# First binary convolution in four 64x64 tiles of TensorE, with halves of images exchanged by DMA

## The chip, the cores and the metric

One core of one Trainium2 chip runs the program. The metric is the time of one execution on the device in microseconds; smaller is better. The engines are TensorE (PE, with its weight loads as PEld), VectorE (DVE), ScalarE (ACT) and GpSimd (POOL); SyncE (SP) issues nearly all DMAs.

## The reference

The input is x, 8 images of 28x28 pixels with 64 channels, in float32. Four blocks follow each other, each as x = x + block(groupnorm(x)), with 32 groups of two channels per image:

```python
x = x + swin_attention(_gn(x))      # shifted 7x7 windows, 8 heads of width 8, relative position bias, mask
# second block, on v = _gn(x) padded by one pixel:
bin_k = where(kernel > 0, 1, -1); alpha = mean(abs(kernel), axis=(0, 1, 2))
bin_x = where(v > 0, 1, -1);      beta = mean(abs(v), axis=channels)
K = sum of beta over 3x3 / 9
x = x + conv3x3(bin_x, bin_k) * (K * alpha) + bias
x = x + conv3x3(_gn(x), sign(kernel2))
x = x + gated_branch(_gn(x))        # 64 -> 2*128 channels, causal conv of 4 taps, silu, gate, 128 -> 64
```

The change touches the second block (a 3x3 convolution of signs, and the scale K * alpha) and the order of some work around it.

## The kernel before

**Layout.** Two images stand on the 128 partitions: channels of the first on 0 to 63, of the second on 64 to 127. The 8 images are four groups g = 0 to 3 of two images. A group has 784 pixels, in two halves i = 0, 1 of 14 rows (392 columns, one PSUM bank in float32).

**Attention** runs over 16 rows of windows R (four per group), each in two parts p; k = 2R + p. Per k: PE multiplies keys and queries (`scores`, L695: four tiles of 32 rows by 49 columns, on row strips 0, 32, 64, 96 and with outputs on partitions 0 or 64 of two banks), DVE takes maximum and difference (`shift`), PE transposes (`turn`), ACT takes exp, PE multiplies with the values (`values`, L726). Then DVE weighs, PE gathers and projects, DVE adds to x (`residual`). POOL masks the keys (`mask_keys`, L207; at the start DVE does one half of the first mask) and ACT seeds the PSUM banks with the position bias. `filler` is a matmul of zeros whose result nobody reads; the numbers of them behind the loads and behind `proj_v(0)` are written in the code (9 and 6).

**First convolution.** `signs(g)` (DVE, L1108) writes +-0.5 into the padded tile sg1. `conv1(g, i)` (PE, L802 to L811) has 9 taps, each one bf16 matmul of 128x128 weights by 392 columns. The weights w1 are block diagonal: a 64x64 block for each of the two images and zeros elsewhere. Output u = 2g + i goes to bank u % 4.

**Channel sums.** ACT writes the absolute normed values (`absolutes`, L500); POOL adds neighbours in the row (`row_sums`, L323 and L325) and in the column (`box_sums`, L330 and L332) into v2. `channel_sums(g, i)` (PE, L859) multiplies v2 with the block diagonal aw (float32, 392 columns; each float32 matmul stands in the trace as two records). ACT copies the result into ka (`evac_ka`, L541).

**finish1(g, i)** (DVE, L1154 and L1156) multiplies the convolution with ka and adds bias and x. It waits for conv_done and ka_ready. When both halves are done, `layer_moments` gives the statistics of the next norm, PE mixes channel pairs (`mix`, L630 and L631), DVE finishes them (`variances`, L996 to L1001) and POOL takes the inverse root (`rsqrt`, L287 and L289).

**Second convolution.** Its input is split in three bf16 parts. ACT makes part one (`split_a`, L550 and L551), DVE the remainder (`remainder`, L1168), ACT part two (`split_b`, L560 and L562), DVE or POOL part three (`third_part`, L220). SP's DMAs place parts in p12 and p33 (L254, L261). PE runs `conv2_stacked` (L823) and `conv2_third` (L837, L842), with 128x64 weights in pairs that write to partitions 0 and 64 of one bank.

**Order.** Each engine runs its list in the order in which it is written; there is no planner. Behind the attention the lists are PE L862 to L898, DVE L1206 to L1255, ACT L590 to L606 and POOL L406 to L418. Waits are on semaphores that count up. SP issues the loads, then the DMAs of the second convolution from the wait for p1_ready on (L244), then the stores.

Of the kernel before, what the change touches and what calls it, by code (L numbers as in the profile page):

```python
# [11 lines left out]
BF16 = mybir.dt.bfloat16  # L12

P = 128
C = 64
HW = 28
TOK = HW * HW
NG = 4
# [10 lines left out]
HALF = TOK // 2  # L29
HR = HW // 2  # L30
# [20 lines left out]
def program(nc, x_in, xw_in, cst_in, wts_in, late_in, ker1_in, ker2_in, rel_in, out):  # L51
    ctx = ExitStack()
    with ctx:
        def sb(name, shape, dt=F32):
            return ctx.enter_context(nc.sbuf_tensor(name, shape, dt))
# [42 lines left out]
        def col(l, g):  # L98
            return l * NG + g
# [24 lines left out]
        v1 = sb("v1", [P, HW, HW])  # L124
        v2 = sb("v2", [P, NG, HW, HW])
        ka = sb("ka", [P, 2, HALF])

        w2 = sb("w2", [P, NTAP, C], BF16)
        parts = sb("parts", [P, 2, 3, PAD, PAD], BF16)
# [21 lines left out]
        def sems(names):  # L151
            return [sem(n) for n in names.split()]
# [27 lines left out]
        sg_ready, ab_ready, h1_done, h_done, v1_done, box_ready = sems(  # L180
            "sg_ready ab_ready h1_done h_done v1_done box_ready")

        conv_done, ka_done, ka_ready, prod_done, x_done = sems("conv_done ka_done ka_ready prod_done x_done")

        p1_ready, rem_ready, p2_ready, p2_placed, p3_ready = sems("p1_ready rem_ready p2_ready p2_placed p3_ready")
# [47 lines left out]
        @block.sync  # L233
        def _(sp):
            sp.dma_start(xwflat[:, 0, :], xw_in[:, 0, :]).then_inc(ld_x0, 16)
            sp.dma_start(wts[:], wts_in).then_inc(ld_w, 16)
            sp.dma_start(rel[:, 0], rel_in).then_inc(ld_rel, 16)
            sp.dma_start(xwflat[:, 1, :], xw_in[:, 1, :]).then_inc(ld_x1, 16)
            sp.dma_start(xwflat[:, 2:NG, :], xw_in[:, 2:NG, :]).then_inc(ld_x2, 16)
            sp.dma_start(xflat, x_in).then_inc(ld_xu, 16)  # L240
            sp.dma_start(ker1[:], ker1_in).then_inc(ld_k1, 16)
            sp.dma_start(ker2[:], ker2_in).then_inc(ld_k2, 16)
            sp.dma_start(late[:], late_in).then_inc(ld_late, 16)
            for g in range(NG):  # L244

                s = g % 2
                if g >= 2:
                    sp.wait_ge(conv_done, 2 * NG + 2 * (g - 1))
                for part, signal in enumerate((p1_ready, p2_ready)):

                    if part == 0 or g > 0:
                        sp.wait_ge(signal, g + 1)
                        for w in range(2):
                            sp.dma_start(p12[64 * part:64 * part + 64, s, w],  # L254
                                         parts[64 * w:64 * w + 64, s, part]).then_inc(stacked[s], 16)
                if g > 0:

                    sp.wait_ge(p3_ready, g + 1)
                    for row in range(2):
                        for w in range(2):  # L260
                            sp.dma_start(p33[64 * row:64 * row + 64, s, w, 0:PAD - row],  # L261
                                         parts[64 * w:64 * w + 64, s, 2, row:PAD]).then_inc(thirds_stacked[s], 16)
            for g in range(NG):
                for i in range(2):

                    sp.wait_ge(res_ready, 2 * g + i + 1)
                    sp.dma_start(out[:, g, i * HALF:(i + 1) * HALF],
                                 res[:, g, i * HALF:(i + 1) * HALF]).then_inc(stored, 16)
            sp.wait_ge(stored, 16 * 2 * NG)
# [151 lines left out]
        def _(act):  # L421
# [114 lines left out]
            def evac_ka(u):  # L536
                i = u % 2
                act.wait_ge(ka_done, u + 1)
                if u >= 2:
                    act.wait_ge(prod_done, u - 1)  # L540
                act.activation(ka[:, i], bk[4 + i][:, 0:HALF], ACT.Identity).then_inc(ka_ready, 1)  # L541
# [46 lines left out]
                act.activation(sz[:, u % 4], zbank(u)[:, 0:HALF], ACT.Silu).then_inc(sz_ready, 1)  # L588

            evac_ka(0)  # L590
            evac_att(NR - 1)
            evac_ka(1)
            evac_ka(2)
            evac_ka(3)
            absolutes(NG - 1)
# [24 lines left out]
        def _(pe):  # L620
# [12 lines left out]
            def filler(ps, n):  # L633

                for _ in range(n):
                    mm = pe.matmul(ps, idle[:, 0:P], idle[:], start=True, stop=True)
                return mm
# [116 lines left out]

            proj_qk(0)
            proj_v(0)
            filler(ps_t[1], 6)
            pe.wait_ge(init_dve, 2)
            scores(0)
            proj_qk(1)  # L760
# [41 lines left out]
            def conv1(g, i):  # L802
# [7 lines left out]
                                   start=(tap == 0), stop=(tap == NTAP - 1))  # L810
                mm.then_inc(conv_done, 1)  # L811

            def conv2_stacked(g, i):

                if i == 0:
                    pe.wait_ge(stacked[g % 2], stacked_by(g))
                    if g == 0:
                        pe.wait_ge(p2_placed, 2)
                ps = conv_bank(2 * NG + 2 * g + i)
                for tap in range(NTAP):  # L820
                    ky, kx = tap // 3, tap % 3
                    for w in range(2):
                        pe.matmul(ps[64 * w:64 * w + 64, 0:HALF], w2[:, tap],  # L823
                                  p12[:, g % 2, w, ky + i * HR:ky + (i + 1) * HR, kx:kx + HW],
                                  start=(tap == 0), stop=False)
# [27 lines left out]
            def channel_sums(g, i):  # L853
                if i == 0:
                    pe.wait_ge(box_ready, g + 1)
                u = 2 * g + i
                if u >= 2:
                    pe.wait_ge(ka_ready, u - 1)
                pe.matmul(bk[4 + i][:, 0:HALF], aw[:], v2[:, g, i * HR:(i + 1) * HR, :],  # L859
                          start=True, stop=True).then_inc(ka_done, 1)  # L860

            pe.wait_ge(w1_ready, 2)  # L862
            conv1(0, 0)
            values(NP - 1)
            project(NR - 2)
            channel_sums(0, 0)
            gather(NR - 1)
            conv1(0, 1)
            project(NR - 1)
            channel_sums(0, 1)  # L870
            conv1(1, 0)
            conv1(1, 1)
            mix(col(1, NG - 1), 1, nth(1, NG - 1), ps_qk)
            channel_sums(1, 0)
            channel_sums(1, 1)
            mix(col(2, 0), 1, nth(2, 0), ps_qk)
            conv1(2, 0)
            conv1(2, 1)
            channel_sums(2, 0)
            channel_sums(2, 1)  # L880
            mix(col(2, 1), 1, nth(2, 1), ps_qk)
            conv1(3, 0)
            conv1(3, 1)
            pe.wait_ge(w2_ready, 7)
            conv2_stacked(0, 0)
            channel_sums(3, 0)
# [82 lines left out]
        def _(dve):  # L969
# [102 lines left out]
            dve.memset(d[:, :, :, WT:64], 0.0).then_inc(init_dve, 1)  # L1072
            dve.wait_ge(pe_bt, 1)
            dve.tensor_tensor(bt[:], ps_o[:, 0:1], ww("bp"), ALU.add).then_inc(bt_ready, 1)
            dve.wait_ge(ld_x1, 16)
            window_moments(1).then_inc(gn_stats, 1)
            dve.wait_ge(ks_ready, 1)
            mask_keys(dve, 0, 0, 2).then_inc(kex_first, 1)
            dve.wait_ge(bt_ready, 1)
            dve.wait_ge(init_dve, 2)  # L1080
            shift(0)
# [126 lines left out]
            residual(NR - 2)  # L1208
            dve.wait_ge(ld_late, 16)
            finish1(0, 0)  # L1210
            residual(NR - 1)
            dve.wait_ge(res_done, NR)
            moments(g, 1).then_inc(gn_stats, 1)
            finish1(0, 1)
            layer_moments(0, 2)
            variances(col(1, g), 1, nth(1, g), ps_qk)
            signs(g)
# [154 lines left out]
```

## Time and profile before

| | |
|---|---|
| median of 3 runs | 218.71 us (217.41 to 220.54) |
| profiled execution, whole time | 217.4 us |
| its span, first to last instruction | 215.5 us |
| PE, DVE, ACT, POOL busy | 203.2, 154.1, 138.9, 94.8 us |
| HBM read, written | 5.03, 1.61 MB |

The span is cut in three here: loads and first norm (to about 13 us), attention (to about 130 us), and the three other blocks. Busy times overlap between engines; a matmul's record runs on while the next one streams, so that the distance between the starts of matmuls, which the chain of waits shows, tells their price, and not the mean length of one.

### The profile page before, as it was taken

What the parts mean: (1) busy time and instruction counts of PE and PEld (TensorE: products, weight loads), DVE (VectorE), ACT (ScalarE), POOL (GpSimd) and SP (SyncE); (2) the same over time, 40 slices, a digit from 0 to 9 for tenths busy, and PEclk for the clock granted to TensorE, in tenths of its full rate; (3) what the DMA queues carried; (4) which work ended last, traced back from release to release, by engine and by line L of the source; (5) the groups of instructions that cost most, each with busy time, mean ns of one, the idle gap of its engine ahead of it and who ended that gap; (6) DMA issues with size and microseconds to landing.
All of it is one profiled execution on the core that took longest, in us unless ns stands there. A gap on an engine that the chain in (4) does not pass through costs nothing.

```text
span 215.5 us, 6793 instructions
## 1 busy us (share of the span) xinstructions
PE 203.2 (94%) x2734; PEld 143.3 (66%) x2735; DVE 154.1 (71%) x316; ACT 138.9 (64%) x294; POOL 94.8 (44%) x108
## 2 busy tenths in 40 slices
PE   7788999999999999999999998997899999899994
PEld 2356888888888878888788865654566665445441
DVE  4665699977886868878769755999796862625543
ACT  2438598779776987788877762278444364876631
POOL 0349999970325199322792019487435200100000
PEclk9999999999999999999999999999999999999999
DMA  6970000000000000000000000001347700002032
GB/s 211 434 292 0 3 3 6 0 3 5 3 3 3 3 2 3 3 3 3 5 0 3 5 3 0 0 22 24 79 94 171 171 2 0 0 3 75 6 111 106
DMA packets 4701, 10.03 MB, mean 47 GB/s; under 512 B 704, under 2 KB 3520, under 8 KB 4544
## 3 DMA queue, kind: packets, MB, share of 16 engines
q1 hardware_dynamic: 4528, 9.27, 13.6%
q8 instruction: 22, 0.36, 0.7%
q10 hardware_dynamic: 144, 0.34, 0.4%
q14 instruction: 7, 0.06, 0.1%
HBM read 5.03 MB, written 1.61 MB: 31 GB/s over the span
## 4 chain that ended last, share of the span: by engine, by line
PE 75%; ACT 7%; DVE 6%; DMA 4%; POOL 3%; issue 3%; SPq 1%; ACTq 0%; POOLq 0%; DVEq 0%
PE turned L706 12%; PE outs L726 11%; PE scores L695 10%; PE scores L914 5%; PE scores L915 4%; PE qkv L666 4%; PE qkv L676 4%; PE scores L808 4%; PE turned L942 3%; PE scores L823 3%; PE outs L748 2%; PE turned L859 2%; DMA xw<-xw_in 2%; DMA p<-parts 2%; PE scores L932 2%
## 5 line engine op out<-in xcount | busy, mean ns | idle before, releaser
L1035 DVE TENSOR_REDUCE mx<-scores 113x16 f32<-113x784 f32 x32 | 30.9, 965 | 9.5 <-PE scores L695 9.3
L706 PE MATMUL turned<-cst,d 113*113 113x113 f32 x256 | 33.3, 273 | 0.9 <-DVE d L1040 0.9
L706 PEld LDWEIGHTS turned<-cst,d 113*113 113x113 f32 x256 | 27.8, 178 | 8.5 <-issue 7.1
L475 ACT ACTIVATE pt<-turned 113x392 f32<-113x392 f32 x64 | 28.4, 495 | 7.1 <-PE turned L706 5.8
L1040 DVE TENSOR_TENSOR d<-scores,mx 113x784 f32<-113x784 f32 x32 | 31.2, 976 | 1.1
L207 POOL TENSOR_TENSOR kex<-ks,cst 128x784 f32<-128x784 f32 (+1 forms) x16 | 23.2, 1452 | 18.6 <-ACT ks L454 18.5
L726 PEld LDWEIGHTS outs<-vsb,pt 113*49 113x49 f32 x1024 | 26.1, 125 | 6.1 <-issue 2.9
L287 POOL TENSOR_TENSOR rstd<-ve,mhalf 128x1 f32<-128x1 f32 (+1 forms) x15 | 8.7, 578 | 47.5 <-DVE ve L1001 47.3
L445 ACT ACTIVATE scores<-rel 113x784 f32<-113x784 f32 x32 | 26.2, 817 | 5.0 <-DMA rel<-rel_in 3.7
L726 PE MATMUL outs<-vsb,pt 113*49 113x18 f32 x1024 | 29.2, 199 | 0.0
L695 PE MATMUL scores<-kex,qs 32*49 32x196 f32 x512 | 28.2, 332 | 0.0
L465 ACT ACTIVATE vsb<-qkv 49x256 f32<-49x256 f32 x32 | 12.8, 399 | 14.4 <-PE qkv L676 14.3
L1185 DVE SCALAR_TENSOR_TENSOR yy<-su,sz 128x392 f32<-128x392 f32 x16 | 8.2, 563 | 18.5 <-PE turned L942 12.5
L581 ACT ACTIVATE su<-scores,late 128x392 f32<-128x392 f32 x16 | 9.3, 587 | 12.8 <-PE scores L915 12.8
L695 PEld LDWEIGHTS scores<-kex,qs 32*49 32x49 f32 x512 | 14.6, 117 | 4.1 <-issue 0.7
L487 ACT ACTIVATE att<-qkv 64x98 f32<-64x98 f32 x64 | 16.2, 253 | 0.6
L914 PE MATMUL scores<-xs,g 128*128 128x392 f32 x32 | 13.7, 510 | 0.6 <-ACT su L581 0.6
L666 PE MATMUL qkv<-xn,wts 128*128 128x196 f32 x64 | 13.6, 336 | 0.0
L823 PE MATMUL scores<-p,w 128*64 128x392 bf16 x144 | 13.2, 334 | 0.1
L915 PE MATMUL scores<-xs,g 128*128 128x392 f32 x32 | 13.1, 491 | 0.0
L808 PE MATMUL scores<-sg,w 128*128 128x392 bf16 x72 | 13.0, 332 | 0.0
L323 POOL TENSOR_TENSOR h<-ab 128x840 f32<-128x840 f32 x4 | 6.3, 1585 | 14.7 <-ACT ab L500 14.6
(121 smaller groups left out, 365.5 us busy)
## 6 DMA issues: line engine op xcount, KB each, us to landing
p<-parts SPq DMA_DIRECT2D x20, 112.5 KB, 2.3
x<-x_in SPq DMA_DIRECT2D x1, 1568.0 KB, 9.8
out<-res SPq DMA_DIRECT2D x8, 196.0 KB, 1.9
xw<-xw_in SPq DMA_DIRECT2D x2, 392.0 KB, 4.7
xw<-xw_in SPq DMA_DIRECT2D x1, 784.0 KB, 6.6
p<-parts SPq DMA_DIRECT2D x6, 108.8 KB, 2.8
ker<-ker_in SPq DMA_DIRECT2D x2, 288.0 KB, 10.1
late<-late_in SPq DMA_DIRECT2D x1, 417.0 KB, 10.7
```

What stands on the lines that cost most here:

```text
L207: return engine.tensor_tensor(kex[:, par, :, a * WT:b * WT], ks[:, a * WT:b * WT].rearrange("p (o t) -> p o t", o=1).broadcast_to([P, 4, n ...
L445: act.activation(o, i, ACT.Identity).then_inc(seeded, 1)
L475: act.activation(pt[0:WK, k % 2, j].rearrange("p n (w t) -> p n w t", w=2), ps_t[j][0:WK, :].rearrange("p (n w t) -> p n w t", n=4, w=2)[: ...
L666: mm = pe.matmul(ps_qk[:, n * RT:(n + 1) * RT], ww(name), rhs, start=True, stop=True)
L695: mm = pe.matmul(ps_s[p][64 * w:64 * w + WT, j, a * 4 * WT:(a + 1) * 4 * WT], qs[q, R % 2, m:m + WT], kex[q, R % 2, :, m:m + WT], start=Fa ...
L706: mm = pe.transpose(ps_t[j][0:WK, n * P:n * P + WK], d[0:WK, k % 2, h:h + 2, :].rearrange("p a b -> p (a b)")[:, 0:WK], ident[0:WK, 0:WK])
L726: mm = pe.matmul(ps_o[64 * w:64 * w + WT, 18 * n:18 * n + 18], pt[0:WK, k % 2, j, 2 * a + hp, WT * w:WT * w + WT], vsb[0:WK, R % 2, 2 * n ...
L808: mm = pe.matmul(ps[:, 0:HALF], w1[:, tap, :], sg1[:, g, ky + i * HR:ky + (i + 1) * HR, kx:kx + HW], start=(tap == 0), stop=(tap == NTAP - 1))
L914: pe.matmul(bk[w][:, 0:HALF], g12[:, w, 0], t[:, SHF + a:SHF + a + HALF], start=True, stop=False)
L915: pe.matmul(bk[w][:, 0:HALF], g12[:, w, 1], t[:, SHF - 2 + a:SHF - 2 + a + HALF], start=False, stop=True).then_inc(u_done, 1)
L1035: dve.tensor_reduce(top, sc, AXX, ALU.max).then_inc(max_done, 1)
L1040: dve.tensor_tensor(d[0:WK, s].rearrange("p (j m) t -> p j m t", j=2)[:, :, :, 0:WT], sc, top.rearrange("p j (m o) -> p j m o", o=1).broad ...
```

## The change

In the first three groups each image has its convolution in two tiles of 64x64: half i = 0 of image w on rows and outputs 64w to 64w + 63, half i = 1 on the other 64 rows. For that its data must lie on the other image's partitions: two DMAs per group copy the lower halves of the signs (sgx) and two those of the box sums (v2x), each crosswise. `conv1_quad(g)` is 36 matmuls in place of 18, `sums_quad(g)` four in place of two. The zero blocks of w1 and aw are not multiplied. Both halves of a group are signalled together. The fourth group stays as it was. PE's list behind the attention is reordered, DVE's and ACT's have one step moved each, and at the start DVE's half of the first mask moves ahead of the statistics of the second group, with 2 fillers in place of 6.

```diff
@@ -124,6 +124,8 @@
         v1 = sb("v1", [P, HW, HW])
         v2 = sb("v2", [P, NG, HW, HW])
         ka = sb("ka", [P, 2, HALF])
+        sgx = sb("sgx", [P, NG - 1, HR + 2, PAD], BF16)
+        v2x = sb("v2x", [P, NG - 1, HR, HW])
 
         w2 = sb("w2", [P, NTAP, C], BF16)
         parts = sb("parts", [P, 2, 3, PAD, PAD], BF16)
@@ -180,6 +182,8 @@
         sg_ready, ab_ready, h1_done, h_done, v1_done, box_ready = sems(
             "sg_ready ab_ready h1_done h_done v1_done box_ready")
 
+        sg_swapped = sems("sg_swapped0 sg_swapped1 sg_swapped2")
+        box_swapped = sems("box_swapped0 box_swapped1 box_swapped2")
         conv_done, ka_done, ka_ready, prod_done, x_done = sems("conv_done ka_done ka_ready prod_done x_done")
 
         p1_ready, rem_ready, p2_ready, p2_placed, p3_ready = sems("p1_ready rem_ready p2_ready p2_placed p3_ready")
@@ -241,6 +245,15 @@
             sp.dma_start(ker1[:], ker1_in).then_inc(ld_k1, 16)
             sp.dma_start(ker2[:], ker2_in).then_inc(ld_k2, 16)
             sp.dma_start(late[:], late_in).then_inc(ld_late, 16)
+            for g in range(NG - 1):
+                sp.wait_ge(sg_ready, g + 1)
+                for w in range(2):
+                    sp.dma_start(sgx[64 * (1 - w):64 * (2 - w), g], sg1[64 * w:64 * w + 64, g, HR:PAD])\
+                      .then_inc(sg_swapped[g], 16)
+                sp.wait_ge(box_ready, g + 1)
+                for w in range(2):
+                    sp.dma_start(v2x[64 * (1 - w):64 * (2 - w), g], v2[64 * w:64 * w + 64, g, HR:HW])\
+                      .then_inc(box_swapped[g], 16)
             for g in range(NG):
 
                 s = g % 2
@@ -588,8 +601,8 @@
                 act.activation(sz[:, u % 4], zbank(u)[:, 0:HALF], ACT.Silu).then_inc(sz_ready, 1)
 
             evac_ka(0)
+            evac_ka(1)
             evac_att(NR - 1)
-            evac_ka(1)
             evac_ka(2)
             evac_ka(3)
             absolutes(NG - 1)
@@ -754,7 +767,7 @@
 
             proj_qk(0)
             proj_v(0)
-            filler(ps_t[1], 6)
+            filler(ps_t[1], 2)
             pe.wait_ge(init_dve, 2)
             scores(0)
             proj_qk(1)
@@ -810,6 +823,20 @@
                                    start=(tap == 0), stop=(tap == NTAP - 1))
                 mm.then_inc(conv_done, 1)
 
+            def conv1_quad(g):
+                pe.wait_ge(sg_swapped[g], 32)
+                ps = [conv_bank(2 * g + i) for i in range(2)]
+                for tap in range(NTAP):
+                    ky, kx = tap // 3, tap % 3
+                    for i in range(2):
+                        for w in range(2):
+                            q = slice(64 * w, 64 * w + 64) if i == 0 else slice(64 * (1 - w), 64 * (2 - w))
+                            rhs = (sg1[q, g, ky:ky + HR, kx:kx + HW] if i == 0 else
+                                   sgx[q, g, ky:ky + HR, kx:kx + HW])
+                            mm = pe.matmul(ps[i][64 * w:64 * w + 64, 0:HALF], w1[q, tap, q], rhs,
+                                           start=(tap == 0), stop=(tap == NTAP - 1))
+                mm.then_inc(conv_done, 2)
+
             def conv2_stacked(g, i):
 
                 if i == 0:
@@ -859,28 +886,33 @@
                 pe.matmul(bk[4 + i][:, 0:HALF], aw[:], v2[:, g, i * HR:(i + 1) * HR, :],
                           start=True, stop=True).then_inc(ka_done, 1)
 
+            def sums_quad(g):
+                pe.wait_ge(box_swapped[g], 32)
+                if g > 0:
+                    pe.wait_ge(ka_ready, 2 * g)
+                for i in range(2):
+                    for w in range(2):
+                        q = slice(64 * w, 64 * w + 64) if i == 0 else slice(64 * (1 - w), 64 * (2 - w))
+                        rhs = v2[q, g, 0:HR] if i == 0 else v2x[q, g]
+                        mm = pe.matmul(bk[4 + i][64 * w:64 * w + 64, 0:HALF], aw[q, q], rhs, start=True, stop=True)
+                mm.then_inc(ka_done, 2)
+
             pe.wait_ge(w1_ready, 2)
-            conv1(0, 0)
+            conv1_quad(0)
             values(NP - 1)
             project(NR - 2)
-            channel_sums(0, 0)
+            sums_quad(0)
             gather(NR - 1)
-            conv1(0, 1)
+            conv1_quad(1)
             project(NR - 1)
-            channel_sums(0, 1)
-            conv1(1, 0)
-            conv1(1, 1)
+            sums_quad(1)
             mix(col(1, NG - 1), 1, nth(1, NG - 1), ps_qk)
-            channel_sums(1, 0)
-            channel_sums(1, 1)
             mix(col(2, 0), 1, nth(2, 0), ps_qk)
-            conv1(2, 0)
-            conv1(2, 1)
-            channel_sums(2, 0)
-            channel_sums(2, 1)
-            mix(col(2, 1), 1, nth(2, 1), ps_qk)
+            conv1_quad(2)
+            sums_quad(2)
             conv1(3, 0)
             conv1(3, 1)
+            mix(col(2, 1), 1, nth(2, 1), ps_qk)
             pe.wait_ge(w2_ready, 7)
             conv2_stacked(0, 0)
             channel_sums(3, 0)
@@ -1072,10 +1104,10 @@
             dve.memset(d[:, :, :, WT:64], 0.0).then_inc(init_dve, 1)
             dve.wait_ge(pe_bt, 1)
             dve.tensor_tensor(bt[:], ps_o[:, 0:1], ww("bp"), ALU.add).then_inc(bt_ready, 1)
+            dve.wait_ge(ks_ready, 1)
+            mask_keys(dve, 0, 0, 2).then_inc(kex_first, 1)
             dve.wait_ge(ld_x1, 16)
             window_moments(1).then_inc(gn_stats, 1)
-            dve.wait_ge(ks_ready, 1)
-            mask_keys(dve, 0, 0, 2).then_inc(kex_first, 1)
             dve.wait_ge(bt_ready, 1)
             dve.wait_ge(init_dve, 2)
             shift(0)
@@ -1208,10 +1240,10 @@
             residual(NR - 2)
             dve.wait_ge(ld_late, 16)
             finish1(0, 0)
+            finish1(0, 1)
             residual(NR - 1)
             dve.wait_ge(res_done, NR)
             moments(g, 1).then_inc(gn_stats, 1)
-            finish1(0, 1)
             layer_moments(0, 2)
             variances(col(1, g), 1, nth(1, g), ps_qk)
             signs(g)
```

## Rows read from the trace of the kernel before

**Rows 1.** The page: busy time by engine, then granted TensorE clock in 40 slices.

```profile
PE 203.2 (94%) x2734; PEld 143.3 (66%) x2735; DVE 154.1 (71%) x316; ACT 138.9 (64%) x294; POOL 94.8 (44%) x108
...
PEclk9999999999999999999999999999999999999999
```

**Rows 2.** Chain of waits behind the attention: start us, length us, engine, line.

```profile
130.03 0.97 issue
...
132.43 1.53 PE scores L808 x9
134.36 0.66 PE turned L859 x2
...
144.29 1.76 DVE rem L1168
146.58 0.56 POOL rstd L287
...
149.40 2.46 POOL v L332
```

**Rows 3.** Chain again, two rates in the attention (x is the count).

```profile
21.85 0.81 PE scores L695 x16
...
24.08 0.68 PE qkv L666 x4
```

**Rows 4.** DVE timeline, 130 to 158: start, length, line, shapes, [idle before].

```profile
132.90 0.57 DVE L1154 TENSOR_TENSOR scores<-scores,ka 128x392 f32<-128x392 f32 x1 [0.74 <-ACT ka L541]
...
134.40 0.80 DVE L1065 SCALAR_TENSOR_TENSOR x<-outs,bt,x 128x100 f32<-128x100 f32 x4 [0.26 <-PE outs L748]
...
140.21 0.16 DVE L996 TENSOR_TENSOR sg<-qkv,epsv 128x3 f32<-128x3 f32 x1 [0.38 <-PE qkv L631]
...
144.20 1.84 DVE L1168 TENSOR_TENSOR rem<-xf,parts 128x784 f32<-128x784 f32 x1
...
157.87 0.92 DVE L1168 TENSOR_TENSOR rem<-xf,parts 128x784 f32<-128x784 f32 x1
```

**Rows 5.** ACT and POOL timelines, 139 to 149, same columns.

```profile
140.54 1.04 ACT L500 ACTIVATE ab<-x,nmr,rstd 128x784 f32<-128x784 f32 x1 [0.17 <-POOL nmr L289]
...
141.72 1.58 POOL L323 TENSOR_TENSOR h<-ab 128x840 f32<-128x840 f32 x1
143.39 1.83 POOL L325 TENSOR_TENSOR h<-h,ab 128x840 f32<-128x840 f32 x1
```

**Rows 6.** PE timeline, 144 to 152, same columns.

```profile
144.81 3.22 PE L808 MATMUL scores<-sg,w 128*128 128x392 bf16 x18
148.08 1.72 PE L823 MATMUL scores<-p,w 128*64 128x392 bf16 x18
151.91 1.58 PE L859 MATMUL turned<-v,aw 128*128 128x392 f32 x4 [2.12 <-POOL v L332]
```

**Rows 7.** Timelines of the head: PE, then DVE, then POOL.

```profile
1.17 4.55 PE L636 MATMUL scores<-idle 128*128 128x512 bf16 x12 [1.17 <-DVE idle L1006]
...
7.13 2.10 PE L636 MATMUL turned<-idle 128*128 128x512 bf16 x9
...
11.48 1.47 PE L636 MATMUL turned<-idle 128*128 128x512 bf16 x5
12.88 0.88 PE L695 MATMUL scores<-kex,qs 32*49 32x196 f32 x16
...
9.67 1.03 DVE L977 BATCH_NORM_STATS2 st<-xw 128x6 f32<-128x392 f32 x2
...
10.87 1.02 DVE L207 TENSOR_TENSOR kex<-ks,cst 128x392 f32<-128x392 f32 x1
...
10.62 0.84 POOL L207 TENSOR_TENSOR kex<-ks,cst 128x392 f32<-128x392 f32 x1 [2.09 <-ACT ks L454]
```

**Rows 8.** DMA issues of the page, then the SP queue's timeline.

```profile
p<-parts SPq DMA_DIRECT2D x20, 112.5 KB, 2.3
...
157.04 2.67 SPq L261 DMA_DIRECT2D p<-parts  x4
```

30

## The prediction

> **What bounds the kernel now.** I read the page first. TensorE is busy 94% of the span, at a granted clock that shows 9 in every slice [rows 1]. That speaks for a TensorE-bound kernel, and for a change that halves TensorE's work. But busy time is no bound, so the second view is the chain of waits behind the attention [rows 2]. There the chain stays on PE from 131 to 141.7 us (the convolutions, at 1.53 us for nine taps, and the channel sums, at 0.66 us for one half), then leaves it: the first remainder on DVE, an inverse root and the box sums of group 3 on POOL, and only with the channel sums of group 3 back to PE, which had idled 2.12 us for them [rows 6]. Third, the timeline of DVE over the same stretch [rows 4]: from 132.90 us to the remainder at 144.20 us it idles twice only, 0.26 us for a projection and 0.38 us for a mix. So PE and DVE run side by side there, both nearly full, and PE's relief is worth what DVE waited for it. Last the head [rows 7]: fillers of TensorE run to 12.88 us, when the first scores start, though DVE's half of the mask was ready at 10.87 + 1.02 = 11.89 us.
>
> **The tiles.** conv1_quad has 36 matmuls of 392 columns. If the four tiles of a tap stream together, a group costs nine steps of 1.53 / 9 = 0.17 us, so 1.53 us where two halves cost 3.06. The trace before has no 64x64 tile. The nearest rows are the scores: four tiles on four row strips, with outputs on two halves of two banks. Their 16 records take 0.81 us, 0.05 us each, where 128x128 matmuls with the same 196 columns take 0.68 / 4 = 0.17 us each [rows 3]: more than three run at once. Pairs that share all rows and differ in the output half also run together: 18 in 1.72 us [rows 6]. The new tiles combine the two. Bounds: 1.53 us a group if loads and streams overlap as there; 36 x 0.05 = 1.82 us if the pace of the scores is a limit per instruction; 3.06 us if only two run at once; 36 x 0.17 = 6.1 us if none do. I take 1.53 plus 0.1 for a change of tile shape (at the scores' start and end about 0.1 us is left over: 0.81 against four streams of 0.17).
>
> The Trainium skill (TensorEngine Tiling (Array Packing), Gotcha 1: PSUM Pressure) says that different row tiles can't access one PSUM bank at the same time. By that the two tiles of a half, which are on different rows and write one bank, would take turns, and a group would cost 3.06 us again. The trace speaks against it: the scores' tiles of row strips 0 and 32 write two halves of one bank and keep the pace above. It stays as a rival below.
>
> sums_quad has four float32 matmuls; four together cost 0.66 us in place of 1.31 (twice the 0.66 of one half [rows 2]); one after the other they would cost 2.6 us. PE saves 3 x (1.53 + 0.66) = 6.6 us in all, if the tiles work.
>
> **What that moves, on the path.** The first quad stands ahead of values(31), where conv1(0, 0) stood, with the same 1.53 us: no gain, and 0.1 us lost to the change of shape, since the chain goes on to weigh(15) (the 0.97 us of issue at 130.03 us [rows 2] is PE waiting for it). sums_quad(0) ends as channel_sums(0, 0) did, again with 0.1 us of shape change, shared with the first one in my sum since DVE's finish1(0, 0) waits for ka (0.74 us idle [rows 4]): together -0.1 us, at worst -0.4 us at the scores' pace. ACT now copies ka twice before evac_att(15), so project(15) comes some 0.4 us later. DVE needs it only behind finish1(0, 1), 0.57 + 0.63 us later than before, so its wait of 0.26 us goes: +0.26 us. If PE were 0.8 us later still, it would come back. Then the moments of group 3 and of group 0, as before. PE has by then done conv1_quad(1) and sums_quad(1) and idles, so both mixes run as soon as their moments stand, and the 0.38 us wait [rows 4] goes too.
>
> What is late next: POOL. Its row sums for group 3 wait for ACT's absolutes at 140.54 us, which wait for the root of variances(1, 3), ahead of the second wait [rows 5]. They gain the 0.26 us and a little, not the 0.64. DVE's remainder(0) took 1.84 us where an undisturbed one takes 0.92 [rows 4]; it ended at 146.04 us, which is 0.82 us after POOL's second row sum (143.39 + 1.83 = 145.22 us [rows 5]). So it stood still until POOL was done, as two engines that lock each other out would, and an earlier start of it buys nothing: it ends when POOL's sum ends, plus 0.82. Behind it come variances(2, 1), the root, the box sums and the channel sums of group 3 [rows 2], from which on the order is unchanged and PE nearly full. The tail therefore gains what the row sums gain: 0.3 us to 0.4 us, less the 0.1 above. I take 0.3, with bounds -0.1 (shape changes at their upper end, gain of 0.26) and 0.7 (both waits, none lost).
>
> mix(2, 1) moves behind conv1(3). PE: quad(2) from about 139.0, sums to 141.2, conv1(3) to 144.2 with 3.06 us; the mix ends before 145.6, when remainder(0) does. It costs nothing; without that cover it would cost up to 1.4 us less whatever PE is early.
>
> **The DMAs.** Twelve more, in SP's list ahead of the wait for p1_ready. An issue takes 2.67 / 4 = 0.67 us of the queue, a landing 2.3 us [rows 8]. Groups 0 and 1 exchange in the middle of the attention, long before use. The signs of group 2 are ready at 127 us and are used at 139. Its box sums end at 136.5 us: two issues, 1.3 us, and 2.3 us to land make 140.1, and sums_quad(2) is due at about 140.5. SP is then free at 137.9 us, before p1_ready at 143 us, so nothing behind is held. If the landing takes 1 us more, PE's slack before the mix covers it; beyond that, it counts in full. Price zero.
>
> **The head.** Four fillers fewer: 4 x 2.10 / 9 = 0.93 us [rows 7]. The mask: DVE and POOL start their halves together; DVE's took 1.02 us for half the elements of a 0.92 us operation, and ended 0.44 us after POOL's (11.46 us), so here too one waited for the other. Moved ahead, it ends at 11.0 us if DVE comes first, at 11.9 us if POOL does; the two remaining fillers end at 11.95 us. Scores start then, 0.93 us earlier. DVE's statistics of group 1 (1.03 us and 0.2 for merging [rows 7]) now stand between: in the worse case they end at 13.1 us, and shift(0), which began at 13.92, starts at 13.15. So 0.8 us, bounds 0.75 and 0.93. Everything in the attention hangs on that first difference, so it moves along; the loads are long in. Sum: 0.8 + 0.3 = 1.1 us less. Against the profiled execution, 217.4 - 1.1 = 216.3 us. That one equals the fastest of the runs shown; their median is 1.3 us higher, so for the median 218.7 - 1.1 = 217.6 us.
>
> **The rivals.**
> *PE was the bound.* For it: 94% busy [rows 1], and the chain of waits on PE until 141.7 us. Then all 6.6 us and the 0.8 come out: 211.3 us. Against it: DVE's two idles sum to 0.64 us there, and PE already idled 2.12 us for POOL. 5%.
>
> *The tiles take turns* (slower side). Place: conv1_quad(0), ahead of values(31), then sums_quad(0). In two turns: 1.53 us more in front of weigh(15), 0.66 us more in front of finish1(0, 0); 1.53 us more before project(15), of which about 0.8 is covered by DVE. It comes to 1.5 + 0.7 + 0.7 less the 1.1: about 219.5 to 220.5 us. It decides once a quad takes over some 2.3 us, where the gain of the head is used up. None at once: 4.6 + 2.0 + 3.5 - 1.1 = 9 us more, 227.7 us. For it: no row shows the four tiles of this shape. 7% and 3%.
>
> *TensorE's clock falls.* PE's work between 135 and 151 us shrinks to islands: idle from about 135.2 to 137.3, and from mix(2, 1) at 144.6 until p12 is placed, about 147.7 us (conv2_stacked started at 148.08 [rows 6]). That is 3.1 us, beyond the longest idle that rows show at full clock, 2.12 us [rows 6]. At the lower clock, as in the first burst, 12 fillers took 4.55 us where nine later took 2.10 [rows 7]: PE lost 4.55 - 12 x 0.233 = 1.75 us until it rose. conv2_stacked(0, 0) would hide a part. Cost 0.5 to 1.8 us: 218.1 to 219.4 us, and in two gaps up to 222. 9%.
>
> *Head gains nothing*, because some load or POOL's list sets the first rows of the attention: 218.4 us. 6%. The forecast itself has 66%; 4% is for what I don't see.
>
> **Numbers.** Predicted 217.6 us. The runs shown spread over 3 us without any change, so the range takes 2.4 us below (runs like the fastest, and 0.7 for the tail) and 2.2 above (the tiles in two turns, or the clock): 215.2 to 219.8. About 2% (4.4 us) is what a measurement of this kernel can tell from no change. Faster by over 2% is the PE-bound rival and a little: 6%. Slower by over 2% needs the serial tiles, or two falls of the clock: 7%. Within: 87%.
>
> **What would show it.** In the trace after: conv1_quad 36 records in about 1.6 us (3.1: turns); scores(0) at about 11.95 us and DVE's first maximum at 13.0 to 13.2; no idle of DVE for PE between 134 and 144 (shifted by 0.8); row sums of group 3 about 1.1 us earlier than 141.72, remainder(0) again ending 0.8 us behind the second; PE idle of 2 us and more in the islands, at clock 1.00; channel sums of group 3 at about 150.8 us. I would be wrong if POOL and DVE take their lock in another order there (each such swap moves 1 to 2 us either way), or if the swap of group 2 lands after 141 us.

## The result: 0.6% slower, and TensorE's clock fell twice

The kernel after takes 219.4 us, median of 12 runs (218.43 to 220.48), against 218.7 us of before beside it. The ratio is 1.0062, 95% interval 1.0037 to 1.0086: slower, by less than 2%, where 217.6 us and a ratio of 0.995 were forecast. The time lies inside the range of 215.2 to 219.8 us, but it moved the other way than forecast. Medians here count every run; ratios leave out runs over 1.5% above the fastest of their kernel. Its profiled execution took 219.4 us at a span of 217.4 us, 1.9 us more than before's.

The page of the kernel after, its busy row and the granted clock in 40 slices:

```profile
span 217.4 us, 6930 instructions
...
PE 201.3 (93%) x2797; PEld 141.4 (65%) x2797; DVE 153.0 (70%) x316; ACT 138.5 (64%) x294; POOL 94.9 (44%) x108
...
PEclk9999999999999999999999999796699999999999
```

TensorE is busy 1.9 us less [rows 1], and the clock row dips to 7 and then to 6 where before's stays at 9. All 12 runs have a granted clock below 1.00 (0.975 to 0.992). The same stretch of the profiled one read by windows (start and end, length, PE busy and its records, granted clock, share of DMA, GB/s), cut where the clock changes:

```profile
core 0: us, PE busy (x), PEclk, DMA share, GB/s
134.80:138.50 3.70, 1.26 (x16) 1.00 0.25 54
138.50:141.90 3.40, 3.40 (x43) 0.50 0.00 0
141.90:148.70 6.80, 5.00 (x42) 1.00 0.16 34
148.70:155.50 6.80, 4.84 (x20) 0.51 0.17 36
155.50:160.00 4.50, 4.50 (x55) 0.99 0.26 57
```

The clock stands at its lower level (1.2 GHz in place of 2.4) from 138.5 to 141.9 us and from 148.7 to 155.5 us. Ahead of the first fall TensorE did little: 1.26 us of records in 3.7 us, and behind the second conv1_quad's sums those are mixes, whose matmuls have one or two columns. Ahead of the second it waited 1.80 us for x, with a mix before that wait. The timeline of PE shows the islands (behind each row the idle time before it, and who ended it):

```profile
136.63 0.38 PE L643 MATMUL qkv<-mv,cst 128*128 128x2 f32 x2 [1.79 <-DVE mv L1016]
...
137.88 0.35 PE L643 MATMUL qkv<-mv,cst 128*128 128x2 f32 x2 [0.65 <-DVE sg L1028]
...
147.72 2.22 PE L850 MATMUL scores<-p,w 128*64 128x392 bf16 x18 [1.80 <-DVE x L1188]
151.91 2.98 PE L886 MATMUL turned<-v,aw 128*128 128x392 f32 x4 [1.96 <-POOL v L345]
```

No idle is longer than 1.96 us, and that one comes behind the second fall; ahead of the falls stand 1.79 and 1.80 us. Before had 2.12 us [rows 6], which went by at full clock in its profiled execution. The chain of waits behind the attention shows what the low clock did:

```profile
126.63 1.65 PE scores L836 x36
...
138.46 3.00 PE scores L836 x36
141.46 0.96 PE turned L897 x8
...
146.58 0.56 POOL rstd L300
...
151.91 2.98 PE turned L886 x4
```

The first quad (126.63) takes 1.65 us for its 36 matmuls, the third (138.46) 3.00 us for the same. The channel sums follow late, then conv1 of group 3 at full clock. The second fall meets the channel sums of group 3: 2.98 us at 151.91, where before's took 1.58 at the same instant [rows 6]. So everything that the head and the order had gained was gone by 146.58 us, where POOL's root starts at the very time of before's [rows 2], and 1.4 us more went in the channel sums. The rest, to 1.9 us, came with the next matmuls.

The head did what the sum said. First scores, DVE's half of the mask, DVE's first maximum:

```profile
11.95 0.88 PE L708 MATMUL scores<-kex,qs 32*49 32x196 f32 x16
...
10.45 0.57 DVE L211 TENSOR_TENSOR kex<-ks,cst 128x392 f32<-128x392 f32 x1 [0.75 <-ACT ks L467]
...
13.00 0.97 DVE L1067 TENSOR_REDUCE mx<-scores 113x16 f32<-113x784 f32 x1 [0.79 <-PE scores L708]
```

12.88 us became 11.95 [rows 7]. DVE got its mask in first and took 0.57 us in place of 1.02.

### The profile page after: what moved, and what is told of

Read it like the earlier page. It is cut to its first block, busy times and chain, and to the rows that moved or that the text cites. A ratio compares the mean times of both kernels' runs of the same rounds, so it can differ in the third digit from the quotient of the medians.

```text
span 217.4 us, 6930 instructions
## 1 busy us (share of the span) xinstructions
PE 201.3 (93%) x2797; PEld 141.4 (65%) x2797; DVE 153.0 (70%) x316; ACT 138.5 (64%) x294; POOL 94.9 (44%) x108
## 4 chain that ended last, share of the span: by engine, by line
PE 72%; DVE 8%; ACT 7%; issue 4%; POOL 3%; DMA 3%; SPq 1%; DVEq 0%; ACTq 0%; POOLq 0%
PE turned L719 12%; PE outs L739 11%; PE scores L708 10%; PE scores L946 5%; PE scores L947 4%; PE qkv L679 4%; PE qkv L689 4%; PE turned L974 3%; PE scores L836 2%; DMA xw<-xw_in 2%; PE outs L761 2%; PE scores L964 2%; ACT pt L488 2%; PE scores L850 1%; PE scores L821 1%
## 5 line engine op out<-in xcount | busy, mean ns | idle before, releaser
L850 PE MATMUL scores<-p,w 128*64 128x392 bf16 x144 | 13.7, 342 | 1.8 <-DVE x L1188 1.8
L689 PE MATMUL qkv<-wts,xn 128*49 128x64 f32 x256 | 10.3, 222 | 2.6 <-ACT qs L468 2.6
```

The source lines that it names most:

```text
L689: mm = pe.matmul(ps_qk[64 * e:64 * e + WT, a * C:(a + 1) * C], xn[:, R % 3, a], ww("wv")[:, e * C:(e + 1) * C], start=True, stop=True)
```

## The experiments

Each kernel ran in up to five rounds beside the kernel before on the same chip; ratios are to that. "Hold" is this function, which reads zeros and writes a bank nobody reads at that time:

```python
def hold(n):
    pe.wait_ge(res_done, NR)
    for _ in range(n):
        pe.matmul(ps_o[:, 0:384], idle[:, 0:P], idle[:, 0:384], start=True, stop=True)
```

### The clock held, and only that

```diff
             sums_quad(1)
+            hold(7)
             mix(col(1, NG - 1), 1, nth(1, NG - 1), ps_qk)
+            hold(3)
             mix(col(2, 0), 1, nth(2, 0), ps_qk)
...
             mix(col(2, 1), 1, nth(2, 1), ps_qk)
+            hold(12)
             pe.wait_ge(w2_ready, 7)
             conv2_stacked(0, 0)
+            hold(10)
```

> The kernel after, with 32 matmuls of zeros (384 columns, bf16, into a bank nobody reads) put on TensorE where it idles: 7 ahead of the mix of group 3's first-block moments, 3 behind it, 12 ahead of the first conv2_stacked and 10 behind it. Nothing else differs. Theory 1, the clock: the granted clock stays 1.00 from 130 to 160 us, the third conv1_quad takes 1.6 us in place of 2.9, channel sums of group 3 start at about 150.6 us, and the time is about 1.2 us below before (ratio 0.993 to 0.996). Theory 2, the order on DVE and POOL or the 12 DMAs took the time and the clock only came along: the time stays at that of the kernel after (ratio about 1.006), or rises by what the added matmuls delay.

Measured: 215.95 us (215.76 to 216.58), ratio 0.9892 (0.9861 to 0.9924), clock 1.00. The same windows (columns as above):

```profile
134.80:138.50 3.70, 3.09 (x26) 1.00 0.25 54
138.50:141.90 3.40, 3.40 (x51) 1.00 0.00 0
141.90:148.70 6.80, 6.19 (x48) 1.00 0.16 36
148.70:155.50 6.80, 6.41 (x54) 1.00 0.31 68
```

And of its chain of waits the root, the channel sums of group 3, and a later DMA:

```profile
145.38 0.56 POOL rstd L300
...
150.72 1.58 PE turned L886 x4
...
157.64 3.88 DMA p<-parts
```

TensorE does 32 useless matmuls more, and the kernel gets 3.4 us faster than without them (219.4 against 215.95, in two sessions, each with before beside it: 1.0062 against 0.9892). So the falls of the clock are what costs, and theory 2, that the order or the DMAs took the time by themselves, is out. (That the order sets how much a fall costs is shown further down.) The channel sums start at 150.72 us; the prediction's signs had 150.8. The ratio is lower than theory 1 said, 0.993 to 0.996, for a reason that the runs of before give, below: they have falls of their own.

### One stretch at a time

The same kernel with the first two holds alone, and with the last two alone.

> The kernel after with the added matmuls of zeros only in the first stretch (7 ahead of the mix of group 3's first-block moments, 3 behind it). The clock theory: the first fall (138.5 us) goes, the second (148.8 us) stays, clock about 0.984 to 0.992 over the span. If the falls cost about the same, about 216.9 us; if the second is the one that counts, since the channel sums of group 3 and what follows run in it, 217.3 us or more (216.0 with both held, 219.4 with none).

Measured: 217.44 us (215.84 to 218.06), ratio 0.9947 (0.9919 to 0.9974), clock 0.992 in the profiled execution.

> The same with the added matmuls only in the second stretch (12 ahead of the first conv2_stacked, 10 behind it). The first fall stays: third conv1_quad 2.9 us, mix of group 1 behind conv1 of group 3 at 145.4 us, box sums at 147.5 as in the kernel after. The 12 matmuls may then stand in the way, since the stretch begins 1.7 us later. About 217.2 to 217.9 us, clock 0.984.

Measured: 217.56 us (216.52 to 219.03), ratio 0.9954 (0.9927 to 0.9981). Its profiled execution, 218.52 us at a clock of 0.983, was one of the longer ones; nine of the 12 have 0.990 to 0.992. With one fall left, either one, the kernel stands 1.5 us (second left) or 1.6 us (first left) above 215.95; with both, 3.4. So by the medians the falls cost about the same, and they add up. The 216.9 us expected for that case were added wrongly: half of 3.4 us on top of 216.0 makes 217.7. The other case, that the second fall is the one that counts, fits the 217.44 us but not the 217.56.

### As many instructions, no work

```diff
-        pe.matmul(ps_o[:, 0:384], idle[:, 0:P], idle[:, 0:384], start=True, stop=True)
+        pe.matmul(ps_o[:, 0:1], idle[:, 0:P], idle[:, 0:1], start=True, stop=True)
```

> The kernel after with the same 32 added matmuls of zeros in the same places, but one column each in place of 384: as many instructions, almost no streaming. The clock theory: the clock falls twice again, time as the kernel after (ratio 1.004 to 1.008). Rival, the added instructions help by their waits or their places in the list and not by TensorE's work: ratio 0.989 again.

Measured: 218.99 us, ratio 1.001 (0.997 to 1.005). The interval excludes the rival's 0.989 and reaches only the lower end of the clock theory's 1.004 to 1.008. The single times say why: 10 of 12 lie between 218.65 and 220.07 us at a clock of 0.976 to 0.984, as the kernel after, and two at 217.18 and 215.96 us with 0.991 and 0.992, near the held ones. In the profile:

```profile
134.80:138.50 3.70, 1.66 (x21) 0.82 0.25 54
138.50:141.90 3.40, 3.40 (x42) 0.50 0.00 0
...
155.50:160.00 4.50, 4.50 (x42) 0.76 0.24 51
```

The clock is down in the first stretch again, here from 137.2 to 144.0 us, and once more behind 154 us. With one column per matmul the falls stayed, with 384 they went. That rules out the holds' places in the list and their waits as the cause of the gain.

### The head alone

```diff
-            filler(ps_t[1], 6)
+            filler(ps_t[1], 2)
...
-            dve.wait_ge(ld_x1, 16)
-            window_moments(1).then_inc(gn_stats, 1)
             dve.wait_ge(ks_ready, 1)
             mask_keys(dve, 0, 0, 2).then_inc(kex_first, 1)
+            dve.wait_ge(ld_x1, 16)
+            window_moments(1).then_inc(gn_stats, 1)
```

> The kernel before with the head of the change alone: DVE's half of the first mask ahead of the statistics of group 1, and 2 fillers in place of 6. Theory 1: the gain of the head, 0.93 us in the trace of the kernel after, reaches the end when the clock stays up: ratio 0.995 to 0.997, clock 1.00 throughout. Theory 2, something later (POOL's list, a load, the box sums) takes it back: ratio 0.999 to 1.001.

Measured: 216.77 us (216.06 to 218.06), ratio 0.9947 (0.9916 to 0.9978): seven of its 11 runs have a clock of 0.999 or 1.00 and a median of 216.45 us, four have 0.992 and 217.64 to 218.06. Before's runs at full clock beside it have a median of 217.21 us, so the head is worth 0.76 us, of 0.8 forecast. Its profiled execution, at a span of 215.8 us, was one of the four, and slower than before's. Windows, and two rows of PE's timeline:

```profile
145.00:148.70 3.70, 3.65 (x31) 1.00 0.04 9
148.70:152.10 3.40, 1.28 (x7) 0.98 0.29 68
152.10:156.00 3.90, 3.90 (x24) 0.58 0.26 59
```

```profile
151.04 2.14 PE L859 MATMUL turned<-v,aw 128*128 128x392 f32 x4 [2.12 <-POOL v L332]
...
153.75 2.46 PE L842 MATMUL scores<-parts,w2z 128*64 128x392 bf16 x18
```

The idle ahead of the channel sums is 2.12 us, to the hundredth that of before [rows 6], where the clock stayed up; here it fell about 1 us after the idle had ended. So one and the same idle can go either way. The clock didn't stay up throughout, as theory 1 had it, and yet the gain came through.

> The kernel after with the head undone (statistics first, 6 fillers). Theory 1: the clock falls behind the attention as in the kernel after, and the time is 0.9 us above it: ratio to before 1.010. Theory 2, the head's fewer fillers bring the fall of the clock: the clock stays 1.00 and the ratio is 0.998 to 1.000.

This is the kernel after with the head as before. Measured: 220.56 us (219.6 to 222.89), ratio 1.0108 (1.0062 to 1.0154), clock 0.976. Taking the head out costs another 1 us and leaves the falls: the missing fillers are not their cause.

### The two heaps of before

The 12 runs of before beside the kernel after are 217.17 to 217.59 us five times and 218.71 us and more seven times, with nothing between. If the upper heap is one fall of the clock in that idle of 2.12 us, matmuls of zeros there take it away:

```diff
             conv2_stacked(0, 0)
+            hold(10)
             channel_sums(3, 0)
```

> The kernel before with 10 matmuls of zeros (384 columns) behind its first conv2_stacked, where TensorE idles 2.1 us ahead of the channel sums of group 3. The times of before fall in two heaps, near 217.3 and near 218.7 us. Theory: the upper heap is one fall of the clock in that idle; then the held kernel has one heap near 217.3 us and a ratio of about 0.997. Rival: the heaps have another cause; then they stay, ratio 1.000.

Measured: 217.62 us, 12 runs from 217.17 to 218.01, ratio 0.9972 (0.9952 to 0.9993), clock 1.00. Of the 29 runs of before beside it, 14 lie at 217.18 to 217.92 and 15 at 218.66 to 220.47. The upper heap is gone. The granted clock of each run says the same: in the three sessions of the experiments, the 40 runs of before with 0.992 or less took 218.50 us and more, the 33 with 0.998 and more took 217.92 us and less. The kernel before itself loses 1.3 us to the clock in about half of its runs; its profiled execution was of the other half.

### What the tiles are worth, with the clock held

> The kernel before with the head of the change and the same 10 matmuls of zeros, no tiles, no exchange, old order. With the clock held in both, the difference to the kernel after with its matmuls of zeros (215.95 us) is what tiles, exchange and new order are worth together: 0.3 us by the prediction's sum (216.3 us here); 0.8 us or more if PE's relief is worth more than DVE's two waits.

Before with the head and hold(10): 217.05 us (216.78 to 217.35), ratio 0.9936 (0.9913 to 0.9958), span 215.1 us.

Next the tiles with the lists of before. The edit to the kernel after, on PE's list (and before's order of residual, moments and finish1 on DVE, evac_ka and evac_att on ACT come back with it):

```diff
-            conv1_quad(1)
             project(NR - 1)
+            conv1_quad(1)
-            sums_quad(1)
             mix(col(1, NG - 1), 1, nth(1, NG - 1), ps_qk)
+            sums_quad(1)
             mix(col(2, 0), 1, nth(2, 0), ps_qk)
             conv1_quad(2)
             sums_quad(2)
+            mix(col(2, 1), 1, nth(2, 1), ps_qk)
             conv1(3, 0)
             conv1(3, 1)
-            mix(col(2, 1), 1, nth(2, 1), ps_qk)
```

> The kernel after with the lists behind the attention in the order of before (residual and moments of group 3 ahead of the second finish1; the quads where the second halves stood, the second one behind the last projection), head as after. Theory 1: TensorE's work is as small as in the kernel after, but spread more evenly; if that is enough the clock stays 1.00 and the ratio is 0.996; if it falls once, 1.000 to 1.003. Theory 2, the new order of DVE and ACT is what costs: ratio 0.996 whatever the clock does.

Without holds: 217.28 us (216.51 to 220.1), ratio 0.9963 (0.9935 to 0.9992). The clock is 0.960 to 0.992 in its 12 runs, so it fell in every one. Two rows of the profiled execution:

```profile
143.41 0.38 PE L643 MATMUL qkv<-mv,cst 128*128 128x2 f32 x2 [1.86 <-DVE mv L1016]
...
143.88 4.86 PE L821 MATMUL scores<-sg,w 128*128 128x392 bf16 x18
```

It fell during conv1 of group 3 (4.86 us, in place of 3.23 in the held kernel), and here the mix of group 1 (143.41) stands ahead of that convolution and didn't wait behind it. The ratio is the second theory's, "0.996 whatever the clock does". So the same tiles, with falls of the clock too, take 217.28 us in the old order and 219.40 us in the new one (in two sessions). The loss of 3.4 us comes with both, the falls and the new order. Which part of the order it takes was not run alone; the traces point at the mix, which in the kernel after stands behind the slowed matmuls.

> The tiles in the order of before behind the attention, head as after, with matmuls of zeros in its idle stretches (6 behind the second sums_quad, 10 behind the third, 10 behind the first conv2_stacked). With the clock at 1.00 it gives the price of the new order alone against the kernel after with its matmuls of zeros: by the prediction's sum the new order is worth 0.3 us, so a ratio of 0.991 to 0.992. Rival: the order is worth nothing, since POOL's and DVE's lock sets the end either way: 0.989.

With holds (6, 10 and 10): 216.99 us, ratio 0.9931 (0.9907 to 0.9955), span 215.1 us. Nine of its 11 runs have a clock of 1.00 and lie at 216.45 to 217.16 us; two stand at 220.48 and 220.57 us with 0.967 and 0.969. So the holds don't keep the clock up every time.

A ratio to before hangs on how many runs of before had a fall. So here are the runs with a clock of 0.998 and more alone, each against before's of the same kind beside it (medians in us, number of runs):

| kernel | its runs | before's | difference |
|---|---|---|---|
| before with hold | 217.62 (12) | 217.54 (14) | +0.08 |
| head alone | 216.45 (7) | 217.21 (11) | -0.76 |
| head, hold | 217.05 (6) | 217.54 (14) | -0.49 |
| head, tiles, old order, holds | 216.88 (9) | 217.32 (8) | -0.44 |
| head, tiles, new order, holds | 215.95 (6) | 217.21 (11) | -1.26 |

Before's own medians differ by 0.33 us between the sessions, so a difference of that size says nothing. In the old order the tiles and the exchange are worth nothing that can be measured. The new order with them is worth 0.5 to 0.8 us on top of the head, more than the 0.3 of the prediction's sum. The rival of the last run, that the order is worth nothing (0.989), lies outside its interval. What the new order would bring without the tiles was not run.

### The root of group 1 first

In the held kernel the remainder of group 0 stands still behind POOL's row sum, and variances, root and box sums behind it. So variances(2, 1) goes first, and its mix moves between the halves of conv1(3); the last hold has 4 matmuls in place of 10:

```diff
             layer_moments(1, 2)
-            remainder(0)
             variances(col(2, 1), 1, nth(2, 1), ps_qk)
+            remainder(0)
...
             conv1(3, 0)
-            conv1(3, 1)
             mix(col(2, 1), 1, nth(2, 1), ps_qk)
+            conv1(3, 1)
```

> The kernel after with the matmuls of zeros (4 in place of 10 ahead of the channel sums of group 3), and variances(2, 1) ahead of remainder(0) on DVE, its mix between the two halves of conv1 of group 3 on TensorE. If the chain there is remainder (held up by POOL), variances, root, box sums, then the box sums start 1.4 us earlier and the end comes 1.1 us earlier: ratio 0.984. Rival: remainder(1) on DVE or the DMAs of the third parts take over at once: ratio 0.989.

Measured: 216.03 us (215.54 to 216.33), ratio 0.9895 (0.9865 to 0.9926), span 214.3 us. At full clock that is 1.29 us below before, where the held kernel has 1.26: nothing, in place of the 1.1 us expected. (The profiled spans, 214.3 and 214.7 us, differ by 0.4, but the held kernel's was the longest of its six.) The root now ran against the remainder, and the third part of group 0 against the box sums. POOL's root and last box sum, then DVE's third part, then the third part in the kernel before:

```profile
144.27 1.15 POOL L300 TENSOR_TENSOR rstd<-ve,mhalf 128x1 f32<-128x1 f32 x1 [0.16 <-DVE ve L1043]
...
147.70 1.85 POOL L345 TENSOR_TENSOR v<-v,h 128x784 f32<-128x784 f32 x1
```

```profile
147.77 2.61 DVE L224 TENSOR_TENSOR parts<-rem,parts 128x784 bf16<-128x784 f32 x1 [0.47 <-ACT parts L575]
```

```profile
148.81 1.35 DVE L220 TENSOR_TENSOR parts<-rem,parts 128x784 bf16<-128x784 f32 x1
```

An undisturbed root took 0.56 us [rows 2]; the third part, 2.61 us here, took 1.35 us before. It ended at 150.38 us, 0.83 us after POOL's box sum (149.55): it stood still behind it, as the remainder had behind the row sum. What was taken from one lock went into two others.

> The kernel before with the head, with variances(2, 1) ahead of remainder(0), and 4 matmuls of zeros behind the first conv2_stacked; no tiles, no exchange. If the tiles are needed for what the last one gains, 0.993; if only DVE's order is, 0.988 (1.1 us below the head with its matmuls of zeros).

The kernel before with the head, the same step on DVE and hold(4): 216.37 us (215.91 to 216.58), ratio 0.991 (0.9881 to 0.994), span 214.5 us. Between its two expectations. At full clock that is 0.95 us below before; with the root behind, and 10 matmuls of zeros, it was 0.49. So here the step is worth some 0.5 us, where it brought nothing behind the tiles. This kernel has no tiles, no exchange and no other new order, and comes to within 0.2% of the best one here.

## Why the prediction was wrong

**The step that failed** is in the rivals: "*TensorE's clock falls*", 9%, "Cost 0.5 to 1.8 us", "and in two gaps up to 222". The sum leaves it out, and the signs have the new idles "at clock 1.00". It was the case that came: the clock fell in both gaps of the profiled execution, and stood below 1.00 in all 12 runs. With matmuls of zeros in the gaps 3.4 us came back, 1.5 and 1.6 us for one gap each, so its size was within the bounds.

Two readings led past it. The first: I compared the longest new idle, 3.1 us by my estimate, with "the longest idle that rows show at full clock, 2.12 us", as if an idle were a safe length or not. The idles ahead of the falls turned out shorter, 1.79 and 1.80 us, and the clock fell all the same, as it did after the very same 2.12 us in the kernel with the head alone. Around them PE did little: between 134.8 and 138.5 us mixes almost alone, which look like work in the busy rows (1.26 us) and stream one or two columns each. The second: I took the profiled execution of before for the kernel. Its clock row is clean, but its median was 1.3 us above it, a gap that I wrote down and called a spread. It was a fall of the clock in about half of the runs, and so a sign that this stretch was at the edge already, ahead of a change that takes 6.6 us of work out of it.

Luck had a part in the size. The upper bound of 1.8 us came from the first burst, called "at the lower clock" there. The windows of before show a granted clock of 1.00 from 1.17 to 5.00 us, so what slowed that burst isn't shown. The median ended inside the stated range because the range's upper part was left for this rival and for the tiles in turns; the sum itself pointed the other way.

**The order made the falls dear.** "It costs nothing" was said of the mix that moved behind conv1(3), on the strength of a cover of 1.4 us at full clock. The low clock used the cover up, and DVE then waited 1.13 us for that mix (below). In the old order the falls cost little (217.28 us).

The Trainium skill (TensorE: Matmul & The Clock Gate, Why this matters for your kernels) advises against idle gaps between bursts of matmuls. The runs agree in the direction: matmuls in the gaps took the falls away. A gap's length alone didn't tell here.

**The tiles: right.** 36 matmuls in 1.65 us where 1.63 was the sum; four tiles run at once. The rule of the Trainium skill cited in the prediction (TensorEngine Tiling (Array Packing), Gotcha 1), that row tiles can't share a PSUM bank at a time, does not show: with turns it would have been 3.06 us. The four matmuls of the first sums_quad took 0.86 us in the chain of waits, 0.2 us more than the 0.66 I took.

**PE's relief moves little: right in the mechanism.** The row sums of group 3 started 1.22 us earlier, at 140.50 where 141.72 stood [rows 5], of 1.1 forecast. The remainder of group 0, after:

```profile
142.50 2.33 DVE L1200 TENSOR_TENSOR rem<-xf,parts 128x784 f32<-128x784 f32 x1
145.96 0.16 DVE L1028 TENSOR_TENSOR sg<-qkv,epsv 128x3 f32<-128x3 f32 x1 [1.13 <-PE qkv L644]
```

```profile
142.17 1.83 POOL L338 TENSOR_TENSOR h<-h,ab 128x840 f32<-128x840 f32 x1
```

It ended at 142.50 + 2.33 = 144.83 us, 0.83 us after POOL's second row sum (144.00), as it had with 0.82 before. DVE's two waits of 0.26 and 0.38 us went. Then comes the new wait, 1.13 us for a mix that stood behind the slowed quad, sums and conv1 of group 3. In the held kernel DVE had no such wait.

**The head: right**, 0.93 us at the first scores where I took 0.8 (DVE's mask came first), and 0.5 to 0.8 us at the end. **The DMAs: right**: sums_quad(2) never waited for them. Two issues took 1.10 us, less than the 1.3 taken.

**The sum, with the clock held: nearly right.** In the held kernel's profiled execution the channel sums of group 3 start 1.19 us earlier than before, of 1.1 forecast, and 0.8 us reach the end of the span; a DMA of third parts took back some (157.64 in its chain: TensorE then waited 0.60 us where before waited 0.24). That execution was the longest of its six; by the medians at full clock the gain was 1.26 us. The term for the order and the tiles, 0.3 us, was too small: 0.5 to 0.8.

## What to carry to other kernels

Work taken off TensorE can cost time through its clock: before thinning a stretch, look at what TensorE still does there; here a stretch that held little but mixes of one and two columns was followed by a fall (at 138.5 us). What a fall costs depends on what stands behind the slowed matmuls in the other engines' lists: the same tiles lost 3.4 us in one order and some 0.5 us in the other (217.28 us without holds, 216.88 with them at full clock). When the median lies above a clean profile and the times come in two heaps, look for a fall of the clock in the upper heap before costing anything in that stretch. A few matmuls of zeros in the waits, in front of nothing that is due, are a cheap test and here also the cure: they were worth 3.4 us, more than the whole change. They were no guarantee: two of 11 runs of one held kernel fell all the same.

## What the runs showed of the hardware

- The granted clock can fall after work has resumed: at 138.5 us with the third quad's first matmuls at 138.4, at 148.8 us where conv2_stacked had run since 147.72, and in the kernel with the head alone about 1 us after the channel sums had begun at 151.04. It can fall in the idle too. In the kernel with the second stretch held it fell at 137.7 us, while TensorE ran nothing:

```profile
137.40:137.60 0.20, 0.05 (x1) 1.00 0.35 79
137.60:137.80 0.20, 0.00 (x0) 0.59 0.88 196
```

- At the lower level four 64x64 tiles took 0.33 us a tap in place of 0.17 to 0.18.
- The same program goes either way from run to run: of 73 runs of before beside the experiments 40 had a fall and 33 had none.
- Four 64x64 tiles with four different moving streams, two of them sharing their rows and two their bank, run at once; 36 matmuls of 392 columns took 1.65 us. Between tile shapes about 0.1 us is lost (1.65 us, where nine steps of 0.17 make 1.53).
